# Short runs of identity products on TensorE while it waits between the stages of a two-layer decoder

## The reference, cut to what matters

```python
x = x + attn(norm(x))            # layer 0: self attention, 16 heads of 8, plus its own input
x = x + xattn(norm(x), ctx)      # layer 0: cross attention, 16 heads
x = x + ffn(norm(x))             # layer 0: 128 -> 512, butterfly, gelu, butterfly, 512 -> 128
x = x + linear_attn(norm(x))     # layer 1: decayed linear attention, 8 heads of 64
x = x + autocorr(norm(x), ctx)   # layer 1: correlation by FFT, 4 best lags, rolled values summed
x = x + moe(norm(x))             # layer 1: 8 experts, 2 per token, at most 308 tokens each
```

## Time and profile before

| what | us |
|---|---|
| median of 3 runs | 600.41 |
| lowest and highest run | 596.93, 601.2 |
| the profiled execution, its own time | 599.32 |
| its span, first to last instruction | 597.2 |
| TensorE busy with products, in the span | 469.0 (79%) |
| TensorE busy with weight loads | 374.5 (63%) |
| VectorE busy | 332.1 (56%) |
| ScalarE busy | 240.4 (40%) |
| GpSimd busy | 209.2 (35%) |

### The profile page before, as it was taken

The page is one execution under the profiler, slowest core; times in us unless marked ns, Lnnn a source line. Parts: engine busy times, 40 slices in busy tenths (PEclk is TensorE's granted clock), DMA queues, the critical chain, the costliest instruction groups (busy, mean ns, idle before and its releaser), DMA issues. The chain is left out here.

```text
span 597.2 us, 13480 instructions
## 1 busy us (share of the span) xinstructions
PE 469.0 (79%) x5103; PEld 374.5 (63%) x5103; DVE 332.1 (56%) x917; ACT 240.4 (40%) x514; POOL 209.2 (35%) x234
## 2 busy tenths in 40 slices
PE   3899999999986978999999988992663332499950
PEld 1587777777763757899988877781553221266630
DVE  5567677777753535666666652637755667011114
ACT  3766666666552326555555522230220000132313
POOL 3556687799133214000000010316430000557750
PEclk9899999999996999999999987997575555599995
DMA  7970312200000002000000003000024000333317
GB/s 234 386 292 6 143 61 61 63 3 2 4 1 1 0 7 76 1 0 0 0 0 0 0 2 88 19 1 0 1 77 134 1 0 0 103 96 106 113 33 211
DMA packets 31461, 34.72 MB, mean 58 GB/s; under 512 B 5562, under 2 KB 25079, under 8 KB 31289
## 3 DMA queue, kind: packets, MB, share of 16 engines
q1 hardware_dynamic: 29208, 29.50, 15.6%
q0 software_dynamic: 2064, 4.60, 2.4%
q10 hardware_dynamic: 144, 0.00, 0.0%
HBM read 28.65 MB, written 5.46 MB: 57 GB/s over the span
## 5 line engine op out<-in xcount | busy, mean ns | idle before, releaser
L473 DVE TENSOR_REDUCE at_nmax<-bank 128x4 bf16<-128x512 f32 x128 | 82.5, 686 | 44.0 <-PE bank L569 44.0
L413 ACT ACTIVATE at_p<-bank 128x512 f32<-128x512 f32 x128 | 69.2, 596 | 38.2 <-PE bank L588 38.2
L95 POOL TENSOR_TENSOR var<-var,eps 128x12 f32<-128x12 f32 (+1 forms) x8 | 1.6, 206 | 176.4 <-DVE var L88 176.4
L1902 POOL DMA_INDIRECT mo_rows<-mo_n_rows,mo_src_row x24 | 23.0, 959 | 71.3 <-POOLq L1610 64.3
L582 PE MATMUL bank<-ident_b,at_nmax 128*128 128x128 bf16 x512 | 42.8, 221 | 4.3 <-DVE at_nmax L473 3.4
L582 PEld LDWEIGHTS bank<-ident_b,at_nmax 128*128 128x128 bf16 x512 | 30.7, 98 | 18.9 <-issue 9.3
L1975 ACT ACTIVATE mo_h<-bank,mo_b 128x308 f32<-128x308 f32 x32 | 16.5, 517 | 47.5 <-PE bank L1938 47.5
L608 PE MATMUL bank<-at_p,at_v 128*32 128x128 f32 x1024 | 34.7, 276 | 0.9 <-DVE x L490 0.9
L1946 PE MATMUL bank<-mo_w,mo_h 128*128 128x128 f32 (+1 forms) x192 | 33.0, 294 | 1.3 <-ACT mo_h L1975 1.3
L1946 PEld LDWEIGHTS bank<-mo_w,mo_h 128*128 128x128 f32 (+1 forms) x192 | 24.3, 173 | 12.1 <-ACT mo_h L1975 5.3
L1081 PE MATMUL bank<-li_v,li_am 128*128 128x65 f32 x256 | 30.4, 272 | 0.5 <-issue 0.5
(11 more groups left out here) (280 smaller groups left out, 1193.1 us busy)
## 6 DMA issues: line engine op xcount, KB each, us to landing
fo_w<-in_up_stages SPq DMA_DIRECT2D x9, 512.0 KB, 9.3
fo_w<-in_down_stages SPq DMA_DIRECT2D x9, 512.0 KB, 4.7
at_k_ctx<-in_ctx_heads SPq DMA_DIRECT2D x1, 4096.0 KB, 23.9
mo_w<-in_L_ffn_W SPq DMA_DIRECT2D x16, 256.0 KB, 3.1
mo_planes<-ro_zeros POOLq DMA_DIRECT2D x1, 2048.0 KB, 9.1
mo_got<-mo_planes SPq DMA_DIRECT2D x8, 256.0 KB, 5.1
x<-in_x SPq DMA_DIRECT2D x4, 256.0 KB, 3.6
au_ctx<-in_ctx SPq DMA_DIRECT2D x4, 256.0 KB, 3.4
```

Of the source, the lines that this page charges most:

```text
L413: act.activation(m.p[:, s % 2, J * g:J * g + J, :], bank_t[g][:, :].rearrange("p (j t) -> p j t", j=J), ACT.Exp, scale=scale).then_inc(exp ...
L473: dve.tensor_reduce(m.nmax[:, J * g:J * g + J], bank_s[g % 2][:, :].rearrange("p (j t) -> p j t", j=J), AX.X, ALU.max, negate=True).then_i ...
L1902: pool.indirect_dma_start(out=rows[0:m, e % 2, r, :], out_offset=None, in_=n_rows, in_offset=bass.IndirectOffsetOnAxis(ap=src_row[0:m, til ...
```

## The change

A helper `spin` issues `n` products of the bf16 identity with itself into 128 columns of a bank that nobody reads at that time. Nobody waits for these products. They stand at fixed places of TensorE's list; in some places new waits hold them back until another engine has come to a certain point, so that they are spread over its work. In all 571 products are issued, 160 of them in the search. Besides, the last step of linear attention is written out, the four transposes of the down weight come ahead of `turn(0)`, and the two correlation products wait until the last projected group has been read (`spectra`), since the bank that the runs are written to has to be free.

```diff
+def spin(core, pe, bank, n):
+    for _ in range(n):
+        pe.matmul(bank[:, 0:128], core.ident_b[:, :], core.ident_b[:, :], start=True, stop=True)
...
+                if i == V:
+                    pe.wait_ge(copied, len(rounds))
+                if i >= V:
+                    spin(core, pe, bank_r, 8)
                 if i >= 1:
                     mix(i)
+                if i >= V:
+                    spin(core, pe, bank_r, 10)
...
-                turn(0)
                 for c in range(CH):
                     mm = pe.transpose(bank_fold[:, c * D:(c + 1) * D], f.down_w[:, c * 128:(c + 1) * 128],
                                       core.ident[:, :])
                 mm.then_inc(folded_turned, 1)
+                spin(core, pe, bank_down[3], 8)
+                turn(0)
+                spin(core, pe, bank_down[3], 8)
                 pe.wait_ge(folded_copied, 2)
...
-                step(B - 1, left=0)
+                attend(B - 1)
+                out(B - 2)
+                numerator(B - 1)
+                spin(core, pe, bank_q, 16)
+                turn_y(B - 1)
+                spin(core, pe, bank_q, 10)
                 out(B - 1)
+                spin(core, pe, bank_q, 24)
...
+                spin(core, pe, bank_vs, 16)
                 transform(0)
...
+                spin(core, pe, bank_zq, 20)
+                pe.wait_ge(odd_done, groups)
+                spin(core, pe, bank_zq, 20)
+                pe.wait_ge(spectra, 5 * groups)
                 for i in range(HALVES):
                     seqs = B // HALVES
                     pe.wait_ge(summed, groups // HALVES * (i + 1))
                     pe.matmul(core.bank[i][:, 0:T],
                               spec[:, seqs * i:seqs * (i + 1), :].rearrange("p b h -> p (b h)"), inv[:, :],
                               start=True, stop=True).then_inc(corr_done, 1)
+                    spin(core, pe, bank_vs, 12)
+                pe.wait_ge(idx, 1)
+                spin(core, pe, bank_vs, 16)
+                pe.wait_ge(w_sum, 1)
+                spin(core, pe, bank_vs, 16)
+                pe.wait_ge(kernels, 4)
+                spin(core, pe, bank_vs, 16)
                 pe.wait_ge(kernels, HALVES * TOP + 2)
...
+                spin(core, pe, bank_vs, 5)
                 pe.wait_ge(k_copied, 1)
...
+                spin(core, pe, bank_vs, 16)
+                pe.wait_ge(y_cos_done, 1)
+                spin(core, pe, bank_vs, 16)
+                pe.wait_ge(y_cos_done, 2)
+                spin(core, pe, bank_vs, 12)
                 inverse(0)
                 for b in range(B):
                     if b + 1 < B:
                         inverse(b + 1)
                     out(b)
+                spin(core, pe, bank_vs, 24)
...
+            spin(core, pe, bank_m, 24)
             turn(0, 0)
...
             pe.wait_ge(made, 2)
+            for k in (1, 5, 9, 13, 17, 20):
+                pe.wait_ge(s, k)
+                spin(core, pe, bank_m, 14)
             with pe.Fori(0, BITS // ROUND) as i:
...
                 mm.then_inc(compared, 1)
+                spin(core, pe, bank_m, 16)
```

## The result

The changed kernel takes 593.88 us (median of 4 runs, 591.85 to 597.17) beside 600.81 of the kernel before in the same session: ratio 0.9899, interval [0.9856, 0.9942] (the ratio is estimated from the runs of both kernels and isn't the quotient of the two medians, 0.9885). The prediction said 592.0, between 587 and 599. The profiled execution took 593.52 with a span of 591.4, against 599.32 and 597.2 before. The same kernel, run once more as an experiment, gave 592.9, ratio 0.9858 [0.9805, 0.9911].

The account below looks back on a forecast made before the run. TensorE was taken to run at half clock where stages hand over and engines wait in turn. Gains of 8.85 less 0.45 for a fall made 8.4, from the median 600.41 to 592.0 us, range 587 to 599.

Parts of the forecast that it names:

- feed forward: Start of feed forward: transposes and two ups at full clock, first up 1.15 earlier, 1.9 us gained.
- linear attention to autocorrelation: Transposes, output products and first transforms at full clock, less 0.8 and 0.55 for runs in the way: 2.05 us gained.
- kernel section, with D: Kernel section: DFT pair 1.0, short transposes and second correlation 0.2, bringing sequences back 1.3: 2.5 us gained.
- route: Route stage: eight transposes would halve but a run delays the turning: 0.2 us gained, bounds -0.3 and 0.7.
- up to the search: 84 products spread over a wait of 8.11 us ahead of the search: nothing gained, bounds -1.6 and 0.
- search: Ten search rounds, each 0.19 us shorter at full clock, added products hidden: 1.9 us gained, bounds -3 and 2.5.
- behind the search: Behind the search, 0.3 us gained as long as the clock stays up.
- a fall on the way: 0.45 us taken off the summed gains for a fall of the clock somewhere on the way.
- the rival of the longer clock: Clock stays up through the route's logits if gaps alone decide: 3 us more, 589; chance 0.08.
- the forecast's case: Added products hold the clock at the stage changes: 8.4 us gained, 592.0; chance 0.62.
- Holding in part: Clock falls in the kernel section, half the search and at feed forward: 4.2 us gained, 596.2; chance 0.22.
- The slow rival: Products don't keep the clock up and delay real ones at barrier, transforms, route and search: 9.3 us lost, 609.7; chance 0.08.

Follow-up runs that it names:

- no_products: The changed kernel's order and waits with every added run set to length 0: 599.05 us, ratio 0.9978.
- after: The changed kernel as first measured and profiled, against the kernel before: 593.88 us, ratio 0.9899.
- again: The changed kernel itself, unaltered, timed and profiled once more: 592.9 us, ratio 0.9858.
- rest_only: The changed kernel without the 84 products ahead of the search and the 160 in its rounds: 592.27 us, ratio 0.9836.
- route: The changed kernel with 24 products added behind each pair of logits in the route loop: 590.5 us, ratio 0.9829.
- experts: The changed kernel with 90 products added ahead of the experts' first transposition: 590.25 us, ratio 0.9819.
- kern: The changed kernel with five runs (10, 12, 12, 10, 8) in the kernel section instead of one of 16: 591.41 us, ratio 0.9865.
- barrier: The changed kernel with two runs cut, 24 to 8 behind linear attention and 16 to 5 ahead of the first transform: 591.65 us, ratio 0.9851.
- groups: The changed kernel with 5 products behind each of the first five real products of autocorrelation groups 1 to 7: 591.64 us, ratio 0.9863.
- more_short: The changed kernel with the edits of barrier and groups, plus more products where the clock still fell: 584.72 us, ratio 0.9749.

## Why the prediction was right, and which terms were not

The total was right, 592.0 against 593.88 and 592.9, and so was its ground: real products between stages at full clock. `no_products` shows that they, not the order, make the gain. That the total came so near is in part luck. In the profiled execution 5.8 was gained where the sum had 8.4: the kernel section with D came out 4.6 short, the search 0.5, and attention took 0.6 more, while the route gave 0.6, the experts 1.3 and the smaller terms 0.7 more than was said, and the sum's own 0.45 for a fall covered some of it. By terms, gains against before:

| term | predicted | measured |
|---|---|---|
| feed forward | 1.9 | 2.1 |
| linear attention to autocorrelation | 2.05 | 1.3 to 2.4 (B and C; after 2.3) |
| kernel section, with D | 2.5 | -2.1 after, 0.5 again, 0.9 rest_only |
| route | 0.2 | 0.8 after, 0.2 to 0.3 in most others |
| up to the search | 0 | 0.0 |
| search | 1.9 | 1.4 to 1.6 |
| behind the search | 0.3 | 0.3 to 0.7 (H) |
| experts | 0 | 0 to 1.4 (I) |
| a fall on the way | -0.45 | contained above |

*Feed forward* came out by its own steps: the first up 1.12 earlier (1.15 said), the two ups 1.82 shorter, of which gelu gains half.

*Linear attention to autocorrelation.* The mechanism was as said, to the two places where runs stand in the way; the barrier's was mis-sized: 0.45 instead of 0.8. The run starts 0.16 before the output products' row ends, and the barrier opens 0.30 behind TensorE's last product, where it opened 0.54 behind VectorE. The run of 16 cost 0.49 (0.55 said), and with both cut C gained 1.94 (2.0 said). What I had not seen is the fall at the start of linear attention: B is 136.95 where the clock doesn't fall (`route`), 136.96 in again, where it falls at 222.74 behind the first projections, and 137.87 in `experts`, where it falls on them, as these rows of again and of `experts` show:

```profile
221.70 1.16 PE L1061 MATMUL bank<-li_nT,li_wk 128*128 128x128 f32 x8 [0.37 <-ACT li_nT L1011]
```

```profile
223.21 2.07 PE L1061 MATMUL bank<-li_nT,li_wk 128*128 128x128 f32 x8 [0.37 <-ACT li_nT L1011]
```

*Kernel section* is the step that failed. I gave 1.0 to the DFT pair because 65 products stood ahead of it, and took the fall there for the smaller chance. In five of eight profiles the pair was slow all the same: TensorE waits 1.40 ahead of the run behind the fourth kernel operation and 1.46 between that run and the transposes, and the clock fell in the second of these waits or just behind it. In again the waits were the same and the clock stayed, so the waits don't decide it alone. In `kern`, with shorter and more frequent runs, the pair was fast and D at 47.13, as in the two other profiles with these runs. The inverse products' term, 1.3 with bounds 0 and 2.6, measured 0.96 (E). That the groups of the autocorrelation could lose the clock stands nowhere in the prediction; in after it cost 3.1 (D 51.36 against 48.30 in `barrier`, the pair slow in both), a third of what the other stages gained.

*Route and the rival of the longer clock.* Without added products in the loop the clock fell by the end of the third turning in each of eight profiles (the wait ahead of it is 2.29 at most), so the forecast's case held; in after, where it fell only as that turning ended, F gained a little more, 0.8. The Trainium skill (TensorE: Matmul & The Clock Gate, "Why this matters for your kernels") wants no long idle gap between bursts. The rows show that this is not enough, as rows of before had: the clock fell at 444.80 behind a wait of 2.29, at 417.60 behind waits of 1.46 and less, and at 373.20 behind none above 0.24 in the rows. But the rival's price was right: with the wait cut to 0.94, `route` gained the 3 us that it named.

*Search.* 0.18 a round was the step's 0.19. In two of the ten rounds of after, and in one of again, the counting products came at half clock and VectorE waited 0.65 as before, hence 1.4 to 1.6. The lower bound, -3 for added products that are late at half clock (0.3 a round), looks much too far: the rounds that followed such a run lost 0.04 (after) and 0.06 at most (`groups`, a wait of 0.53). No run has the added products in a search wholly at half clock.

*Rivals.* Holding in part describes the mechanism best: there were falls in the kernel section, the search and the autocorrelation. In after they cost 4.6, no less than its 4.2, at other places (D 51.36 against 47.11 in `more_short`, and 0.35 in the search); in again they cost less than half of that. Feed forward, one of its losses, held in each of eleven profiles. That the time was the forecast's and not its 596.2 is due to the gains beyond the sum that are named above. The slow rival fell: the runs in the way cost 0.9 together.

*Signs.* Of the prediction's signs of being right, the two ups (1.96), the last output products (1.16), the barrier that opens because of TensorE and VectorE's wait in the search (0.47) came true; a clock of 1.00 from 355 to the correlations did not in after. Of its signs of being wrong, the DFT pair near 2.07 came in five of eight profiles, but with 3.4 to 6.8 us of half clock and not a whole section; rounds longer than 2.8 came too, two of 2.81 in after (the fifth round is longer in every kernel, 3.24 before and 3.07 after).

## What to carry to other kernels

Where engines pass work back and forth, short dense runs into a free bank, placed inside the waits, keep TensorE's real work at full speed; here they gave 1% as the change had them, and 2.5% once more of the waits were filled. Look at the waits ahead of real products (here 1.3 to 2.3 in the route, 1.4 and 1.5 in the kernel section, 8.5 ahead of the experts), fill them with runs that are shorter than the wait, and trim those that stand ahead of a barrier: `barrier` and `route` show both sides. Judge such a change by its stages over several profiles, since a fall of the clock comes in some executions of a kernel and not in others.

## What was not expected of the hardware

- The clock fell while no row shows TensorE idle for more than 0.24 us at a time (373.20 in after; by their starts the projections came 0.60 apart instead of 0.22), in three of seven profiles of that code. Whether the products of `groups` prevent it stays open.
- The same code had the DFT pair at 1.13 in one execution (again) and at 2.08 in another (after), and the clock came back 3.0 to 6.0 us into the experts. The spread of a single stage, 1 to 3 us, is as large as most terms of the sum.
- Sixteen added products at half clock, 1.89 us of them, cost the next search round only 0.04 of VectorE's wait (0.51 instead of 0.47): they end just as its first products are wanted.
